# Two shared slots for turned probabilities in a quantised cross-attention stage

## The reference, cut to what matters

```python
q = _fq_sym(q, axis=-1); k = _fq_sym(k, axis=-1); v = _fq_sym(v, axis=2)
attn = jnp.einsum('bhqd,bhkd->bhqk', q, k)
attn = jax.nn.softmax(attn.astype(jnp.float32), axis=-1)
attn = _fq_unsigned(attn, axis=-1)      # s = max/255; round(attn/s)*s
out = jnp.einsum('bhqk,bhkd->bhqd', attn, v)
return out @ Wp + bp
```

## Time and profile before

| | us |
|---|---|
| median of 3 runs | 1096.11 |
| lowest and highest run | 1092.66, 1096.12 |
| the profiled execution's own time | 1096.11 |
| span of its trace | 1094.3 |
| PE busy in the span | 1025.5 (94%) |
| DVE busy | 729.5 (67%) |
| ACT busy | 365.2 (33%) |

### The profile page before, as it was taken

One profiled execution on the slowest core, in us unless ns is written; L12 is line 12 of the kernel. 1 busy time (PEld: TensorE's weight loads), 2 busy tenths in 40 slices (PEclk: granted clock), 3 DMA queues, 4 the chain that ended last, 5 costly groups with the idle time before them and its releaser, 6 DMA issues.

```text
span 1094.3 us, 20855 instructions
## 1 busy us (share of the span) xinstructions
PE 1025.5 (94%) x7909; PEld 669.5 (61%) x7909; DVE 729.5 (67%) x1930; ACT 365.2 (33%) x657; POOL 158.0 (14%) x148
## 2 busy tenths in 40 slices
PE   6999999998799887898999999999999998988988
PEld 4776766764335543365777777776767676644444
DVE  4767777677688646586676767676776768454244
ACT  1333333334348701432343333333333332111104
POOL 0000000001000010242222222232323221000000
PEclk9999999999999999998999999999999998999899
DMA  7101001002339986940000000000000002314320
GB/s 276 40 20 39 19 22 36 19 5 93 135 77 192 184 295 229 312 155 1 1 2 1 1 0 0 0 0 0 0 0 0 1 1 78 133 41 167 155 93 3
DMA packets 69161, 77.33 MB, mean 71 GB/s; under 512 B 52592, under 2 KB 59504, under 8 KB 65648
## 3 DMA queue, kind: packets, MB, share of 16 engines
q1 hardware_dynamic: 68672, 75.93, 22.1%
q10 hardware_dynamic: 432, 0.64, 0.2%
HBM read 63.65 MB, written 0.07 MB: 58 GB/s over the span
## 4 chain that ended last, share of the span: by engine, by line
PE 72%; DVE 12%; issue 6%; ACT 4%; POOL 3%; DMA 2%; SPq 0%; DVEq 0%; POOLq 0%
PE ps L2177 15%; PE ps L2138 12%; PE ps L1462 8%; PE ps L2167 7%; PE ps L1452 4%; PE ps L1473 4%; PE ps L1496 2%; PE ps L1508 2%; ACT vals L1998 2%; POOL x_sum L2702 2%; DMA x_keys<-vals 2%; DVE S L2393 1%; PE ps L501 1%; PE ps L1856 1%; PE ps L2746 1%
## 5 line engine op out<-in xcount | busy, mean ns | idle before, releaser
L2177 PE MATMUL ps<-vals,S 128*128 128x257 f32 x784 | 188.8, 384 | 0.7 <-ACT S L2627 0.7
L2138 PE MATMUL ps<-keysT,row_biases_sb 128*128 128x512 f32 (+1 forms) x416 | 187.0, 575 | 0.1
L2702 POOL TENSOR_TENSOR x_sum<-x_max,consts 128x4 f32<-128x4 f32 (+1 forms) x104 | 133.6, 1285 | 324.7 <-DVE x_max L2381 324.7
L2393 DVE SCALAR_TENSOR_TENSOR S<-ps,x_sum,keysT 128x128 f32<-128x128 f32 x392 | 110.8, 344 | 72.3 <-PE ps L2177 63.9
L2177 PEld LDWEIGHTS ps<-vals,S 128*128 128x128 f32 x784 | 143.5, 192 | 19.1 <-issue 1.0
L2627 ACT ACTIVATE S<-S 128x512 f32<-128x512 f32 (+1 forms) x104 | 62.7, 606 | 219.2 <-DVE S L2428 218.7
L2167 PE MATMUL ps<-x_q,x_keys 128*128 128x128 f32 x784 | 113.2, 286 | 0.0
L2138 PEld LDWEIGHTS ps<-keysT,row_biases_sb 128*128 128x128 f32 x416 | 76.8, 192 | 57.2 <-issue 52.1
L2167 PEld LDWEIGHTS ps<-x_q,x_keys 128*128 128x128 f32 x784 | 95.6, 191 | 0.0
L1462 PE MATMUL ps<-ring,S 128*128 128x512 f32 x196 | 92.5, 594 | 0.2 <-DVE ps L1603 0.2
L501 PE MATMUL ps<-consts 128*128 128x512 bf16 x335 | 84.2, 383 | 1.9 <-DVE vals L1939 0.2
(11 more groups left out here) (445 smaller groups left out, 1399.5 us busy)
## 6 DMA issues: line engine op xcount, KB each, us to landing
ring<-weights SPq DMA_DIRECT2D x24, 1024.0 KB, 5.3
keysT<-ctxT SPq DMA_DIRECT2D x2, 3136.0 KB, 14.8
vals<-ctxN SPq DMA_DIRECT2D x1, 6272.0 KB, 22.8
S<-ctxT SPq DMA_DIRECT2D x12, 512.0 KB, 3.9
keysT<-weights SPq DMA_DIRECT2D x6, 864.0 KB, 8.7
ring<-weights SPq DMA_DIRECT2D x6, 768.0 KB, 6.9
ring<-weights SPq DMA_DIRECT2D x2, 864.0 KB, 5.4
row_biases_sb<-row_biases SPq DMA_DIRECT2D x1, 1416.0 KB, 11.7
```

What stands on the lines that cost most here:

```text
L2138: ins = pe.matmul(ps[:, c % 3, 0:width(c)], x2_wk[:, k, :], ctxT[:, k, span(c)], start=k == 0, stop=k == KT - 1)
L2177: ins = pe.matmul(bank(6, D + 1), S[:, a:a + TILE], ctx_and_ones[:, SUB * c + s, :], start=c == 0 and s == 0, stop=c == NC - 1 and s == su ...
L2393: ins = dve.scalar_tensor_tensor(S[:, a:a + TILE], ps[:, 3 + c % 2, 128 * s:128 * s + 128], x2_inv[:, c % 2, s:s + 1], x2_tile_const, ALU. ...
L2702: pool.tensor_tensor(x2_inv[:, c % 2, 0:n], x2_var[:, c % 2, 0:n], C("neg_half").broadcast_to([128, n]), ALU.pow)\
```

## The change

The tile `wide` keeps its two places of 768 columns, but they no longer belong to quarters 0 and 1: quarters 0, 1 and 3 of all pairs now take turns in them. Quarter 2 keeps its place, and the score row no longer holds a turned quarter. The new function `x1_slot` gives the slot and the weigh that last read it. In the sequence of turns without quarter 2, turn number m waits for the weigh of number m-2. So turn (j, 0) waits for weigh (j-1, 1), turn (j, 1) for weigh (j-1, 3), turn (j, 3) for weigh (j, 0), and turn (j, 2) as before for weigh (j-1, 2). `score` of quarter 3 now waits, as the other quarters do, only for the turn that read the score row two pairs earlier.

```diff
--- before.py
+++ after.py
@@ -1805,16 +1805,18 @@
             a, n = X1_FROM[e], TILE * X1_TILES[e]
             return x1_scores_of[j % 2][:, a:a + n // 2]
 
+        def x1_slot(j, e):
+
+            if e == LAST_IN:
+                return keys_room[:, 0:64 * X1_TILES[e]], PROB_GROUPS * (j - 1) + e + 1 if j > 0 else None
+            order = [(p, q) for p in range(j + 1) for q in range(PROB_GROUPS) if q != LAST_IN and (p, q) <= (j, e)]
+            m = len(order) - 1
+            before = PROB_GROUPS * order[m - 2][0] + order[m - 2][1] + 1 if m >= 2 else None
+            return wide_flat[:, 768 * (m % 2):768 * (m % 2) + 768], before
+
         def x1_probsT(j, e):
 
-            a, n = X1_FROM[e], TILE * X1_TILES[e]
-            if e == PARTS - 1:
-                place = x1_scores_of[j % 2][:, a + n // 2:a + n]
-            elif e == LAST_IN:
-                place = keys_room[:, 0:n // 2]
-            else:
-                place = wide_flat[:, 768 * e:768 * e + n // 2]
-            return cut(place.bitcast(mybir.dt.float16), X1_TILES[e], 128)
+            return cut(x1_slot(j, e)[0].bitcast(mybir.dt.float16), X1_TILES[e], 128)
 
         def x1_turned(j, e):
 
@@ -1823,8 +1825,9 @@
         def x1_turn(sp, j, e):
 
             sp.wait_ge(sem("x1_exp"), since("x1_exp", PROB_GROUPS * j + e + 1))
-            if j > 0 and e < PARTS - 1:
-                sp.wait_ge(sem("x1_weighed"), since("x1_weighed", PROB_GROUPS * (j - 1) + e + 1))
+            before = x1_slot(j, e)[1]
+            if before is not None:
+                sp.wait_ge(sem("x1_weighed"), since("x1_weighed", before))
             sp.dma_start_transpose(x1_probsT(j, e), x1_probs(j, e).bitcast(mybir.dt.float16)).then_inc(x1_turned(j, e)[0], 16)
 
         def x1_tensor(pe):
@@ -1931,10 +1934,8 @@
 
             def score(j, b):
                 dve.wait_ge(sem("x1_scores_psum"), since("x1_scores_psum", PARTS * j + b + 1))
-                if j >= 2 and b < PARTS - 1:
+                if j >= 2:
                     dve.wait_ge(*x1_turned(j - 2, b))
-                elif j >= 2:
-                    dve.wait_ge(sem("x1_weighed"), since("x1_weighed", PROB_GROUPS * (j - 1)))
                 at, a, n, out = x1_bank(j, b), X1_FROM[b], SCORED * TILE, x1_scores_of[j % 2]
                 ins = dve.tensor_scalar(cut(out[:, a:a + n], 3, 512), ps[:, at:at + 3, :], 1.0, NEG, ALU.mult, ALU.max,
                                         accum_out=x1_max[:, b:b + 1])
```

## The result

| kernel | median us | runs | range us | ratio to the kernel before |
|---|---|---|---|---|
| before | 1094.53 | 20 | 1088.64 to 1097.94 | |
| changed | 1100.51 | 20 | 1094.73 to 1106.10 | 1.0052 (95%: 1.0036 to 1.0067) |

The change makes the kernel 0.52% slower, some 5.7 us. The forecast was 3.4 us slower (1099.5 us, counted from a median of 1096.11).

The account below looks back on a forecast made before the run. It took DVE's wait for a weigh to close the 8.71 us cycle of a pair. The stage 2.5 us late plus 0.9 us for late-landing turns made 3.4 us on 1096.11: forecast 1099.5 us, own range 1098 to 1101.

Parts of the forecast that it names:

- What bounds the kernel now: Mid-stage: DVE's fourth score waiting for a weigh closes the 8.71 us cycle of a pair; without it 8.08 us.
- The one wait that costs: Mid-stage: only turn (j, 1), now waiting for weigh (j-1, 3), is late; the other new waits cost nothing.
- Release, 0.96 us: First part of the new chain: from the start of weigh (j-1, 3) to the issue of turn (j, 1), 0.96 us.
- H(5): Handover of pair 5, the mark for timing pairs: start of weigh (4, 3), at 363.10 in the kernel before.
- Landing, 3.4 and 3.8: Turn (j, 1) from issue to landing: 3.4 us in even pairs, 3.8 in odd ones, bounds 3.4 and 5.0.
- From weigh (j, 1) to the next handover, 4.28: Second half of a pair's cycle, up to the start of weigh (j, 3): 4.28 us without PE's wait for DVE.
- Middle 0.84: Five pair steps in the stage's middle, three of them odd, come out 0.84 us late in all.
- collisions: Whole stage: turns that land late, perhaps through instruction fetches, now fall on the path; 0.9 us, bounds 0 and 3.6.
- End 1.7: From the start of weigh (5, 3) to the stage's last weigh: 1.7 us of the 2.5 us lateness.
- The rival with the clock: Stage's end: PE's idle gaps lower the clock to 1.2 GHz, 2 us more, 1101.5 us; chance 0.13.
- only the end is late: Rival: landings are short, so the middle loses nothing and the end 1.2 us instead of 2.5; 1097.3 us; chance 0.20.
- The freed DVE sets the pace: Rival: turns land within 2.8 us of issue, so a pair's cycle is 8.08 us; 3.8 us gained, 1092.3; chance 0.08.

Follow-up runs that it names:

- run 1: Kernel before, with a room of its own in the weights' ring for quarter 3's turns, so DVE's wait for the weigh is gone; ratio 0.9951.
- run 3: Kernel before, with one late wait added: turn (j, 1) waits for weigh (j-1, 3) instead of weigh (j-1, 1); ratio 1.0052.
- run 2: Changed kernel with DVE's old wait put back, its fourth score waiting for the weigh two pairs back; ratio 1.0037.
- run 10: The changed kernel profiled and timed once more, with nothing altered; ratio 1.0055 to the kernel before.
- run 7: Kernel before, with turn (j, 1) waiting for weigh (j-1, 3) in pairs 1 to 5 alone; ratio 1.0030.
- run 6: Kernel before, with turn (j, 1) waiting for weigh (j-1, 3) in the last two pairs alone; ratio 1.0011.
- run 8: Changed kernel with 12 more filler matmuls between weigh (j, 0) and weigh (j, 1) at the stage's end, where PE sat idle; ratio 1.0043 to the kernel before.
- run 5: Kernel before, with turn (j, 1) waiting for weigh (j, 0), one weigh later than in the change; expected 1.5% over the kernel before, measured ratio 1.0281.
- run 4: Kernel before, with turn (j, 1) waiting for weigh (j-1, 2), one weigh earlier than in the change; ratio 0.9999.

## Why the prediction was right, and where its sizes were off

The direction, the place and the mechanism held. The result of 1100.5 lies 1 us above the forecast and within its own range (1098 to 1101). That closeness is in part luck: the forecast added 3.4 us to 1096.11, the median of three runs, while the kernel before has 1094.53 over 20, and the change cost 5.7. Both terms for the stage, middle and end, were too small. Point by point:

- *What bounds the kernel now.* Shown right: without the wait the cycle is 8.05 (forecast 8.08), by run 1.
- *The one wait that costs.* Shown by run 3 (same ratio) and run 2 (nothing gained by the relief). "The removed wait pays for most of the new one" was a wrong way to put it: the relief and the chain are alternatives, of which the longer counts.
- *Release, 0.96 us.* Measured 0.9: H(5) 363.48 to turn (5, 1) at 364.4.
- *Landing, 3.4 and 3.8.* Too short. In the changed kernel turns (j, 1) took 4.3, 3.6, 3.8, 3.4 and 4.3. The 4.3 of pair 5 came again in run 10, that of pair 1 did not. Turn (3, 1), turn (5, 1), and turn (4, 2), each with the ns that SP was held, the time of issue and the us to landing:

```profile
L1831 SPq DMA_TRANSPOSE wide<-vals x1: 1425/1425/1425, 345.5 to 345.5; - x1
DMA to landing us min/median/max: 3.8/3.8/3.8
L1831 SPq DMA_TRANSPOSE wide<-vals x1: 1423/1423/1423, 364.4 to 364.4; - x1
DMA to landing us min/median/max: 4.3/4.3/4.3
L1831 SPq DMA_TRANSPOSE x_keys<-S x1: 1540/1540/1540, 356.1 to 356.1; - x1
DMA to landing us min/median/max: 5.5/5.5/5.5
```

- *From weigh (j, 1) to the next handover, 4.28.* Measured 4.38 in four pairs (331.26 to 335.64). In pair 4 it took 5.42, as weigh (4, 2) waited 0.98 us for its turn, 5.5 us in flight. The stretch of 355 to 362 (the rate in 40 slices, and the instruction queue) holds one instruction packet, and inside that flight the transfer rate is at 10 GB/s or less for some 1.5 us:

```profile
GB/s 0 0 0 0 79 278 291 290 291 288 291 288 143 132 262 285 281 291 291 287 291 267 85 293 263 178 63 4 0 0 0 1 7 9 10 10 168 293 290 290
...
q8 instruction: 1, 0.02, 1.4%
```

  That fits a fetch that holds up the turns; it was not tested by itself.
- *Middle 0.84.* Measured 3.6, 2.5 and 2.7 (changed, again, run 7). This is the term that was most mis-sized. Of the 2.8 us that are missing in the first profile, 1.2 are the longer landings of the turns (j, 1), 1.1 the late turn (4, 2), and 0.4 the 4.38 in place of 4.28. I had put such delays under "collisions" at 0.9 for the whole stage. They are nearer to 2 in the middle alone.
- *End 1.7.* Measured 3.8 with a fall of the clock (5.1 in run 10, with the longer fall), 2.7 without (run 6). The extra us at full clock lies ahead of weigh (6, 3): weigh (6, 1) came 4.76 us after H(6) in run 6, not 4.36, and from it to weigh (6, 3) PE took 3.87, not 3.14, with a wait of 0.28 for turn (6, 2) in it. From weigh (6, 3) to the last weigh, 8.53 us, the forecast (8.65) was good.
- *The rival with the clock* (chance 0.13, 2 us) came true in the changed kernel both times, besides the forecast and not in its place. Its price is 1.0 to 1.7 us for the fall of 3.4 us (run 8), near the 2 that I had put. I gave it too little: the gap that I had worked out myself (2.8 us, it was 3.4) was a sign, though not a sure one, as run 6 shows.
- *What I had not seen*: DVE's wait for turn (j, 1), of up to 0.7 us in odd pairs. It cost nothing, as PE has no gap behind it.
- *Rival "only the end is late"*: excluded by run 7. *The freed DVE sets the pace*: right for run 1, where nothing else is added; here no turn (j, 1) landed in under 3.4 us. What I wrote there on a higher transfer rate was wrong. The 0.8 us that I took off belong to a turn at 211 GB/s, which would then land in 3.0 us; the turns of even pairs move at about 290 already (below) and would gain 0.3, by the same estimate, and land in 3.1. Neither is under the 2.8 us that this rival needs.
- *Sum.* The stage's 7.4 us is more than the 5.7 timed (3.9 to 7.3 by the interval). The span shows 4.3, as the earlier fall of the clock near 293 us is missing from it. What of the difference between 7.4 and 5.7 is chance and what is given back later stays open.

## What to carry to other kernels

Before a buffer is shared among more users, look for the wait that moves, not for the one that goes: count from the release of the slot, through issue and landing of the transfer, to its use, and compare with the work that lies between in program order. If the chain is longer by a microsecond, the relief on another engine is worth nothing. And look for free columns in tiles that are only half used at that time: here 768 columns in the weights' ring gave the relief without the cost, 0.49% faster than before and 1% faster than the change.

## What the runs showed of the hardware

- A gap on PE can cost more than its length. With the wait one weigh later the clock averaged 0.66 to 0.87 over the middle, and the time rose by 2.8%, where the chain at full clock, by the expectation of run 5, makes some 1.5%.
- The length of one gap does not tell whether the clock falls: 3.24 us of idle PE left it full (run 6), while 2.67 us (run 7), 2.98 us (run 4) and 3.41 us (changed) had a fall beside or behind them.
- Turns of even pairs move at about 290 GB/s (slices of 355 to 362 above), those of odd pairs mostly at 211. The two differ in the tile they read, but that alone is not the cause: turn (5, 0) of the changed kernel reads the tile of the odd pairs and moved at about 290 too. The rates of 361 to 365.2, in which the rest of turn (4, 3) and the whole of (5, 0) move, 0.65 MB:

```profile
GB/s 10 10 10 139 288 283 293 288 295 290 288 281 271 290 288 285 293 293 288 293 293 285 280 278 261 57 83 0 0 0 0 0 0 0 0 0 0 0 0 0
```

  What makes the difference was not tried.
